# Top-32 attention: 22 wide segments instead of 32 for the first maxima, and a shorter exact path

## The reference

```python
scores = einsum('bthd,bghd->bhtg', Q, K) / sqrt(DH)      # 4096 x 3202 for each of 4 heads
topv, topi = jax.lax.top_k(scores, K_TOP)                # K_TOP = 32
probs = softmax(topv, axis=-1)
attn = zeros_like(scores).at[..., topi].set(probs)
attn_mean = attn.mean(axis=heads)
c_t = attn_mean @ (x_vision @ Wv)
```

## Time and profile before

| | us |
|---|---|
| median of 3 runs (lowest, highest) | 4269.23 (4267.5, 4271.36) |
| the profiled execution, and its span | 4266.21, 4264.4 |
| busy: PE, DVE, ACT, POOL | 3337.1, 3241.3, 2284.6, 1425.2 |

### The profile page before, as it was taken

One profiled execution on the slowest core, in us unless ns is written; L12 is line 12 of the kernel. 1 busy time (PEld: TensorE's weight loads), 2 busy tenths in 40 slices (PEclk: granted clock), 3 DMA queues, 4 the chain that ended last, 5 costly groups with the idle time before them and its releaser, 6 DMA issues. The chain is left out here.

```text
span 4264.4 us, 55224 instructions
## 1 busy us (share of the span) xinstructions
PE 3337.1 (78%) x16624; PEld 2225.8 (52%) x16624; DVE 3241.3 (76%) x8831; ACT 2284.6 (54%) x3031; POOL 1425.2 (33%) x1265
## 2 busy tenths in 40 slices
PE   7665858888888888876757778568999999936776
PEld 3343535555555555544545555357777777712333
DVE  7699999999999999986889999334443434369996
ACT  4574858887778888882323333223332332337774
POOL 0022424444444444443551010023233323205664
PEclk9756767777777777778978998889999999968888
DMA  8600000000000000002212343444433333330111
GB/s 321 242 6 9 10 5 9 9 9 12 9 11 9 9 9 9 9 7 90 67 33 52 88 104 86 119 138 144 124 129 123 126 116 92 121 92 26 54 49 53
DMA packets 263808, 291.04 MB, mean 68 GB/s; under 512 B 55450, under 2 KB 177436, under 8 KB 262368
## 3 DMA queue, kind: packets, MB, share of 16 engines
q1 hardware_dynamic: 240504, 255.10, 19.6%
q10 hardware_dynamic: 19976, 17.80, 1.5%
q0 software_dynamic: 3040, 14.94, 0.9%
HBM read 219.34 MB, written 68.45 MB: 67 GB/s over the span
## 5 line engine op out<-in xcount | busy, mean ns | idle before, releaser
L1061 PE MATMUL score<-KT,q 64*128 64x512 f32 (+1 forms) x1792 | 669.9, 522 | 276.5 <-ACT S L918 159.8
L815 DVE MAX8 cand<-S 128x8 f32<-128x100 f32 (+1 forms) x4096 | 680.4, 245 | 69.9 <-ACT S L918 50.2
L1061 PEld LDWEIGHTS score<-KT,q 64*128 64x128 f32 x1792 | 439.6, 264 | 509.5 <-ACT S L918 219.6
L1089 PE MATMUL up<-ctx,attnT 128*128 128x384 f32 (+1 forms) x1664 | 614.1, 518 | 0.0
L918 ACT ACTIVATE S<-score 128x1024 f32<-128x1024 f32 (+1 forms) x512 | 406.6, 832 | 107.3 <-PE score L1061 107.3
L820 DVE SCALAR_TENSOR_TENSOR S<-S,tops,E 128x3202 f32<-128x3202 f32 x128 | 449.4, 3553 | 10.6 <-ACT E L949 10.6
L1089 PEld LDWEIGHTS up<-ctx,attnT 128*128 128x128 f32 (+1 forms) x1664 | 324.3, 205 | 210.4 <-issue 55.5
L2150 DVE TENSOR_TENSOR ff_gelu<-ff_whole,ff_gelu 128x512 fp32r<-128x512 f32 x128 | 98.3, 768 | 429.5 <-ACT ff_gelu L2277 429.5
L927 ACT ACTIVATE E<-S,below 128x3202 bf16<-128x3202 f32 x128 | 379.7, 2966 | 26.1 <-issue 11.7
L949 ACT ACTIVATE E<-S,ebias 128x3202 f32<-128x3202 f32 x128 | 379.7, 2967 | 1.0 <-DVE S L820 0.7
L2386 PE MATMUL ff_acc<-ff_W,ff_gelu 128*128 128x512 f32 x1024 | 344.4, 397 | 0.0
(11 more groups left out here) (359 smaller groups left out, 6278.0 us busy)
## 6 DMA issues: line engine op xcount, KB each, us to landing
s_hankel<-scratch_K SPq DMA_DIRECT2D x128, 256.0 KB, 4.5
ff_w_low<-scratch_w1l SPq DMA_DIRECT2D x112, 256.0 KB, 2.6
ff_w_low<-scratch_w2l SPq DMA_DIRECT2D x112, 256.0 KB, 2.7
xt_prep<-in_x SPq DMA_DIRECT2D x8, 1024.0 KB, 8.6
scratch_xt<-xt_prep SPq DMA_DIRECT2D x8, 1024.0 KB, 8.3
next_prep<-in_ffn_w_t POOLq DMA_DIRECT2D x8, 1024.0 KB, 11.3
q<-scratch_qt SPq DMA_DIRECT2D x128, 64.0 KB, 1.9
mod_xt<-scratch_xt SPq DMA_DIRECT2D x32, 256.0 KB, 2.7
```

The costliest lines, as they stand in the source:

```text
L815: nc.vector.max(cand[:, h, 8 * k:8 * k + 8], S[:, b, h, k * SEG:end])
L1061: last = nc.tensor.matmul(score[k % 2][:, j % 2, 0:w], lhsT=q[at, part, h // 2, :], rhs=KT[at, h // 2, chunk(j)], start=(part == 0), stop= ...
L1089: last = nc.tensor.matmul(up[:, 0:DV], lhsT=attnT[0:w, e, c - 4 * g, :], rhs=ctx[0:w, c, :], start=(c == 0), stop=(c == GC - 1))
```

## The change

The row is now cut into 22 segments: 21 of 146 columns and one of 136. The candidates of a head are 176 instead of 256. The exact path no longer begins with a MAX8 over the whole row but takes the eight largest that `thresholds` has left in `tops` (these are the row's eight largest whatever the segments are), so it makes three MAX8 and four MATCH_REPLACE. For head 0, which is alone in its `thresholds`, `below` is made by a tensor_scalar, whose second operand is one value for each partition, instead of by a scalar_tensor_tensor with two tensors.

```diff
-SEGS = 32
-SEG = G // SEGS
+SEGS = 22
+SEG = -(-G // SEGS)
 CAND = SEGS * 8
@@ segments
                     for k in range(SEGS):
-                        end = (k + 1) * SEG if k < SEGS - 1 else G
-                        nc.vector.max(cand[:, h, 8 * k:8 * k + 8], S[:, b, h, k * SEG:end])
+                        nc.vector.max(cand[:, h, 8 * k:8 * k + 8], S[:, b, h, k * SEG:min((k + 1) * SEG, G)])
@@ exact
                     for r in range(TOP // 8):
-                        nc.vector.max(tops[:, b, h, 8 * r:8 * r + 8], src)
-                        dve.drain()
+                        if r > 0:
+                            nc.vector.max(tops[:, b, h, 8 * r:8 * r + 8], src)
+                            dve.drain()
                         nc.vector.match_replace(rest, tops[:, b, h, 8 * r:8 * r + 8], src, LOWEST)
@@ thresholds
-                    nc.vector.scalar_tensor_tensor(below[:, at], least, -1.0 + 2.0 ** -23, margin[:, at], ALU.mult, ALU.max).then_inc(s["below_ready"], 1)
+                    if len(heads) == 1:
+                        nc.vector.tensor_scalar(below[:, at], least, -1.0 + 2.0 ** -23, margin[:, at], ALU.mult, ALU.max).then_inc(s["below_ready"], 1)
+                    else:
+                        nc.vector.scalar_tensor_tensor(below[:, at], least, -1.0 + 2.0 ** -23, margin[:, at], ALU.mult, ALU.max).then_inc(s["below_ready"], 1)
```

## The result

The changed kernel takes 4290.53 us (median of 5 runs, 4283.08 to 4292.66) against 4269.23 for the kernel before. The ratio is 1.0047, with a 95% interval of 1.0033 to 1.0062: slower by 0.5%, 21.3 us. The forecast was 4286.5. The profiled execution of the changed kernel took 4290.65 us, with a span of 4288.9.

A forecast was written before the change was run, and what follows sets the result against it. The prediction took ACT's and PE's stretches together to bound the loop, with DVE's saving covered. 33.0 - 10.3 - 2.4 - 2.8 = +17.5 us on the profiled 4266.2 gave 4283.7, 4286.7 as median, forecast 4286.5; range 4260 to 4302.

The forecast's parts named there:

- ACT's stretch and PE's stretch: In attention's loop, 17.3 us of ACT plus 33.9 us of PE make the whole 51.2 us tile, without DVE.
- the third run: Exact path runs once more, for row 2811, head 1, tile 21, nine of its 32 largest in one segment: +33.0 us.
- The two old runs: Exact path's existing runs, for near ties in tiles 2 and 5, lose a 3.56 us pass and start earlier: -10.3 us.
- Start and end: Attention's first and last tiles, where ACT or PE waits for DVE: -2.4 us at the start, -2.8 at the end.
- The loop didn't get shorter: Rival: PE's wait for POOL in the loop lies on the path, so about 4218 us, or 4252 for half; chance 0.12.
- the 1.0 us of room on PE's second score group: In the loop, PE's second score group is ready 1.0 us before ACT needs it, so ACT covers PE's wait for POOL.
- The clock didn't move: Rival: PE's clock rise shifts by 2 us in each tile; 4312 if later (chance 0.08), 4260 if earlier (0.04).
- the fixed cost of an instruction: DVE's fixed time per MAX8 in a row: 62 ns by the trace, saving 0.62 us a head; 156 by the skill.
- The 3.3 us at the start of attention: Gain at attention's start if the skill's 156 ns held, instead of 2.4 us; in all 4285.5 instead of 4286.5.
- My 17.5: Sum of the four terms on the path, 33.0 - 10.3 - 2.4 - 2.8 = +17.5 us over the kernel before.

The follow-up runs named there:

- The shifted boundaries: The changed kernel with segment boundaries moved by 8 columns so row 2811 has at most eight of its 32 largest in one segment: 4252.4 us, ratio 0.9966.

## Why the prediction was right

*The bound.* The step that carried the forecast was that ACT's stretch and PE's stretch add up to a tile and that DVE isn't in the sum. It held from both sides: 3.49 us more DVE a tile changed nothing in the changed kernel, and 1.33 us less ACT gave 36 us. (PE's part of the sum is read from its gapless stretch and from ACT's waits for it; no run changed PE's work.) DVE's busy time in the window from 198 to 1982 us (busy us and instructions of each engine, clock, DMA), before:

```profile
198.00:1982.00 1784.00, 1414.75 (x4429) 889.71 (x4430) 1621.92 (x5687) 1331.45 (x1574) 684.74 (x695) 0.73 0.04 13
```

and after:

```profile
198.00:1982.00 1784.00, 1405.23 (x4416) 889.22 (x4416) 1470.81 (x4405) 1328.45 (x1569) 681.05 (x690) 0.73 0.03 10
```

DVE's is 151 us less, although the third run put some 31 us of work in. The loop made waiting of it.

*The third run.* +33.0 was forecast and +33.1 measured in its tile. The shifted boundaries and the 20 segments show that the row counts decide it. That the size came out so near is in part luck: ACT's wait was 34.52 us and not 32.8, 1.5 us of it was made up within the tile, and the two tiles behind it cost 1.0 us that the forecast had not in it: 34.1 in all.

*The two old runs.* -10.3 was forecast, the waits shrank by 8.1 and the tiles by 7.2 net. The pass that goes was right (3.56). The earlier start was mis-sized: I had 2.2 and 1.0 us, and it was 0.6 and none. (From the flags to the first operation it was 4.87 us in the second run before and is 4.32; in the first it was 1.56 and is 1.55.) From the flags (538.22 + 0.18 = 538.40) to the first operation are 4.3 us of loads and branches for head 3, where I had taken the 2.36 us of idle time in the earlier trace rows for all of it. The rest had been hidden beside the MAX8 of the segments, and came into the open once these were early. The same miss makes the second run's own price 34.4 and not 32.8; for the third, head 1, it is 2.7 us from the flags to the first operation.

*Start and end.* -2.4 and -2.8 forecast, -2.1 and -2.9 measured. In the last tile ACT no longer waits for the edge at all.

*Rivals.* The loop didn't get shorter; the 1.0 us of room on PE's second score group was real. The clock didn't move: from 640 to 1330 us the granted clock is 0.75 on average, against 0.76, and in the tile shown it is 0.57 in the first 12.7 us of PE's long stretch (from 1078.61) and 1.00 in the 20.5 behind, where the earlier trace rows has 0.55 and 1.00. On the fixed cost of an instruction the row was right: 22 MAX8 take 4.75 us, 4.72 by the 62 ns of the row. The 156 ns of the Trainium skill (VectorE: DVE Perf Modes, "The TRN2 errata") would by estimate have made the saving 1.6 us a head; it was 0.6. That figure comes near the fixed part of a single recorded duration here (296 - 146 x 1.048 = 143 ns), but in a row these overlap. (The 3.3 us at the start of attention, worked out from it, would also have been more than the 3.15 us of idle time there.)

*Left over.* My 17.5 against 24.4 in the profiled execution: 3.1 us from the two old runs, 1.0 in the loop behind the third run, and 2.8 behind attention, which I can't assign. Between forecast and median it is only 4.0, because the profiled execution of the kernel before lay 3.0 us below its median and that of the changed kernel did not. That is luck.

## What to carry to other kernels

An engine that is busy 93% of a loop need not bound it. Look for the two engines whose waits for each other tile the loop's period, and try the suspect with extra work before making it faster. A fast path that falls back on data has a price that can be counted beforehand, from the inputs: here one of 16384 pairs of row and head cost 34 us, more than all the rest of the change brought. And when an engine has been freed, the gain is in giving it work from the one that bounds; which piece moves matters, since a piece may be covering a handshake.

## What the runs showed of the hardware

- The scalar_tensor_tensor on one column took 160 ns in tile 0, where POOL was idle, and 641 to 1009 ns in the other 31 tiles, with POOL adding beside it (954 in the mean of all). The tensor_scalar that took its place took 213 to 216 ns with POOL adding and 214 without.
- A tensor_scalar with an accumulator over 3202 columns takes 3548 ns on DVE, and the accumulator's read 83 more. It ran beside POOL's adds, which kept their 7.87 to 7.88 us for seven chunks (7.87 before).
- From the flags to the first operation of the exact path it took DVE 1.55 us for head 0, 2.4 to 2.7 for head 1, 3.2 for head 2 and 4.3 to 4.4 for head 3, where DVE was idle beforehand (changed kernel and 20 segments).
- DVE idles at its loop's jump back, six times of six: 2.3 to 2.4 us in the kernel before, 3.1 to 3.4 in the changed one, 4.2 to 4.5 with 20 segments, 4.6 to 4.8 with the exact path's edit alone, at most 0.03 with a 3.49 us MAX8 as the last instruction ahead of the jump.
